# A four-layer residual network on one core: the residual kept doubled, ScalarE's gates opened in two parts, GpSimd's products held, another load order

## The reference

```
x = x + ssm(x)                       # conv over 16 rows of cond, softplus/tanh gates, a scan over time, 64 states
x = x + lstm(x, h0=cond)             # 512 steps; a = x_t Wx + h Wh + b; c = f c + i g; h = o tanh(c)
x = x + r * y                        # r = sigmoid(xr wr^T), xr = x + (xprev - x) maa_r
                                     # y: each token of xk = x + (xprev - x) maa_k through one of 16 experts
ax = abs(x); p = ax / sum_t(ax); pi = exp(2 p); th = pi / sum_t(pi)
chosen = sum_t(cumsum_t(th) + 0.001 <= cond); level = ax[chosen]
x = x + x * (ax >= level)            # so: x times 2 or times 1
```

## Time and profile before

| what | value |
|---|---|
| time, median of 3 | 4191.82 us (4191.44 to 4198.04) |
| profiled execution | 4197.63 us, of which span 4194.9 us |
| PE busy | 3890.3 us, 93% |
| DVE busy | 3109.5 us, 74% |
| ACT busy | 1679.4 us, 40% |
| POOL busy | 289.2 us, 7% |
| DMA | 267 MB, mean 64 GB/s |

### The profile page before, as it was taken

The page is one execution under the profiler, slowest core; times in us unless marked ns, Lnnn a source line. Parts: engine busy times, 40 slices in busy tenths (PEclk is TensorE's granted clock), DMA queues, the critical chain, the costliest instruction groups (busy, mean ns, idle before and its releaser), DMA issues. The chain is left out here.

```text
span 4194.9 us, 112126 instructions
## 1 busy us (share of the span) xinstructions
PE 3890.3 (93%) x44034; PEld 2542.4 (61%) x44034; DVE 3109.5 (74%) x10143; ACT 1679.4 (40%) x5296; POOL 289.2 (7%) x410
## 2 busy tenths in 40 slices
PE   3999999999999999999999999999599999996885
PEld 3566666666656666665666666665277888783332
DVE  9888888888878888887888888865455544544887
ACT  3334333334333333433333443333244434443554
POOL 2000000000000000000000000000000000002433
PEclk8999999999999999999999999999899999998887
DMA  7111111111111111111111111101233343324432
GB/s 282 27 37 27 27 34 27 34 37 27 27 35 27 32 34 31 27 34 27 27 32 38 27 27 34 22 17 20 79 148 121 139 158 122 120 83 148 148 133 71
DMA packets 388634, 266.97 MB, mean 64 GB/s; under 512 B 289721, under 2 KB 323001, under 8 KB 385060
## 3 DMA queue, kind: packets, MB, share of 16 engines
q1 hardware_dynamic: 366416, 184.21, 16.4%
q0 software_dynamic: 17696, 66.79, 4.2%
q10 hardware_dynamic: 4020, 9.10, 0.6%
HBM read 176.48 MB, written 83.92 MB: 62 GB/s over the span
## 5 line engine op out<-in xcount | busy, mean ns | idle before, releaser
L387 PE MATMUL bank<-buf,buf 128*16 128x256 f32 x32768 | 1874.2, 380 | 67.0 <-DVE buf L704 57.8
L387 PEld LDWEIGHTS bank<-buf,buf 128*16 128x16 f32 x32768 | 906.0, 97 | 890.8 <-DVE buf L704 88.9
L837 PE MATMUL bank<-buf,buf 128*128 128x256 f32 (+1 forms) x3072 | 1037.1, 338 | 4.0 <-DVE buf L1008 2.7
L838 PE MATMUL bank<-buf,buf 128*128 128x256 f32 (+1 forms) x3072 | 979.0, 319 | 0.0
L839 PE MATMUL bank<-buf,buf 128*128 128x256 f32 (+1 forms) x3072 | 978.4, 318 | 0.0
L597 DVE SCALAR_TENSOR_TENSOR buf<-buf,buf,buf 128x256 f32<-128x256 f32 x1920 | 870.9, 481 | 3.2 <-issue 3.2
L682 DVE STREAM_TRANSPOSE buf<-bank 128x256 f32<-128x256 f32 x1024 | 459.4, 449 | 421.7 <-PE bank L387 386.8
L554 ACT ACTIVATE buf<-buf 128x96 f32<-128x96 f32 x1024 | 290.5, 284 | 1146.5 <-DVE buf L687 1146.0
L837 PEld LDWEIGHTS bank<-buf,buf 128*128 128x128 f32 x3072 | 582.0, 189 | 254.6 <-issue 216.3
L839 PEld LDWEIGHTS bank<-buf,buf 128*128 128x128 f32 x3072 | 583.9, 190 | 41.2
L838 PEld LDWEIGHTS bank<-buf,buf 128*128 128x128 f32 x3072 | 584.7, 190 | 38.5
(11 more groups left out here) (137 smaller groups left out, 2977.4 us busy)
## 6 DMA issues: line engine op xcount, KB each, us to landing
buf<-in_wk SPq DMA_DIRECT2D x16, 2048.0 KB, 9.5
buf<-in_wv SPq DMA_DIRECT2D x16, 2048.0 KB, 9.3
buf<-in_xT SPq DMA_DIRECT2D x62, 496.0 KB, 3.8
buf<-in_xT SPq DMA_DIRECT2D x32, 512.0 KB, 3.6
expert_in_scratch<-buf POOLq DMA_DIRECT2D x16, 1024.0 KB, 22.7
x_scratch<-buf SPq DMA_DIRECT2D x32, 512.0 KB, 9.2
buf<-expert_in_scratch SPq DMA_DIRECT2D x16, 1024.0 KB, 11.5
expert_out_scratch<-buf POOLq DMA_DIRECT2D x64, 256.0 KB, 4.7
```

The source lines that it names most:

```text
L387: last = mm(gate_ps[hf][32 * j:32 * j + B, 0:HCOLS], hist[:, k, at_step(slot_at)], wh[:, k, j * GCOLS + hf * HCOLS:j * GCOLS + (hf + 1) * ...
L837: nc.tensor.matmul(out, left[0], right[0], start=first, stop=False)
L838: nc.tensor.matmul(out, left[0], right[1], start=False, stop=False)
```

## The change

The residual. From the first layer on, `stream`, x2 in DRAM and x3 are held doubled. To get there the output weights and bias of the first layer are doubled (`wo_pair`, `wo_rest`), x1 becomes 2 x center + out, the halo of the first tile is 2 x cond, and what reads the doubled x is halved: the scale of ScalarE's `keep_inputs`, maa_k and maa_r (`maa_last` = 0.5 maa, `maa_now` = 0.5 - 0.5 maa). Then `hist` (2h) is added as it is: `keep_x2` is one tensor_tensor over all four blocks, and x2_done counts 1 for it where it counted 4 (all waits on it are divided accordingly). In the finish the second half of `combine` is a plain addition and the multiplier is max(ax >= level, 0.5).

The input. `center` is loaded from a second copy of x, `xB`, which has the tile's steps innermost, batch by batch; the conv's window still reads `xT`.

The finish. ScalarE opens the gates 0 and 1 of row i+2 before `take_sides(i)` and the gates 2 and 3 after `absolute(i+1)`; in the run-in `exponent(0)` stands before the gates of row 1. GpSimd waits once for all four multipliers of a row, and then makes its four products. maa_r is loaded first, ScalarE no longer waits for wr, and the loads of rows 3 to 5 wait for the weighing of rows 0 to 2.

```diff
@@ -200,7 +200,7 @@
                     sp.sem_inc(s["sp_passed"], 1)
-                sp.dma_start(center, x_dram[:, :, bass.ds(m * LTILE, LTILE)]).then_inc(s["center_landed"], 16)
+                sp.dma_start(center, ins["xB"][:, :, bass.ds(m * LTILE, LTILE)]).then_inc(s["center_landed"], 16)
 
@@ -305,11 +305,11 @@
             pool.dma_start(y_d[E * CAP:E * CAP + 1, :], zeros[0:1, 0:D]).then_inc(s["zero_stored"], 16)
-            g.tensor_copy(stream[0][:, :, :, 0], cond).then_inc(s["halo_ready"], 1)
+            g.tensor_scalar(stream[0][:, :, :, 0], cond, 2.0, None, ALU.mult).then_inc(s["halo_ready"], 1)
 
...
                 if later(n, 1):
-                    pool.wait_ge(s["x2_done"], 2 * KD * n)
+                    pool.wait_ge(s["x2_done"], 2 * n)
                     pool.sem_inc(s["pool_passed"], 1)
@@ -489,17 +489,19 @@
                 a(xw[par][:, :, q, :], xw_ps[q % 2][:, 0:LTILE].rearrange("p (b t) -> p t b", b=B), ACT.Identity,
-                  bias=bias[:, q:q + 1]).then_inc(s["xw_ready"], 1)
+                  bias=bias[:, q:q + 1], scale=0.5).then_inc(s["xw_ready"], 1)
 
...
                     act.wait_ge(s["rows_turned"], r)
+                if not later(m, 1):
+                    act.wait_ge(s["share_ready"], 2)
                 act.wait_ge(s["halo_ready"], m + 1)
-                act.wait_ge(s["x2_done"], KD * (r + 1))
+                act.wait_ge(s["x2_done"], r + 1)
                 for k in range(KD):
                     a(mix[:, k, :].rearrange("p (b t) -> p b t", b=B), stream[four][:, k, :, 8 * u:8 * u + 8],
-                      ACT.Copy, scale=maa_k[:, k:k + 1])\
+                      ACT.Copy, scale=maa_last[:, k:k + 1])\
                         .then_inc(s["weighed"], 1)
@@ -519,8 +521,8 @@
             a(y_high[N_STATE:], ones[N_STATE:], ACT.Copy).then_inc(s["y_ones"], 1)
-            a(wo_pair, wo, ACT.Copy).then_inc(s["wo_high"], 1)
-            a(wo_rest[N_STATE:], bo_rows[N_STATE:], ACT.Copy).then_inc(s["wo_high"], 1)
+            a(wo_pair, wo, ACT.Copy, scale=2.0).then_inc(s["wo_high"], 1)
+            a(wo_rest[N_STATE:], bo_rows[N_STATE:], ACT.Copy, scale=2.0).then_inc(s["wo_high"], 1)
             for i, src in enumerate((dt_log, a_log)):
@@ -647,19 +649,17 @@
                     dve.wait_ge(s["halo_ready"], m - 2)
-                v.tensor_tensor(stream[four][:, two(q), :, 1:], out_ps[q].rearrange("p (k b t) -> p k b t", k=2, b=B),
-                                center[:, two(q), :].rearrange("p k (t b) -> p k b t", b=B),
-                                ALU.add).then_inc(s["x1_ready"], 1)
+                v.scalar_tensor_tensor(out=stream[four][:, two(q), :, 1:].rearrange("p k b t -> p (k b) t"),
+                                       in0=center[:, two(q), :].rearrange("p k (b t) -> p (k b) t", b=B), scalar=2.0,
+                                       in1=out_ps[q].rearrange("p (n t) -> p n t", t=LSTEPS), op0=ALU.mult,
+                                       op1=ALU.add).then_inc(s["x1_ready"], 1)
 
...
                 dve.wait_ge(s["h_ready"][1], LSTEPS * n + 8 * u + 9)
-                for k in range(KD):
-                    kept = stream[four][:, k, :, 8 * u + 1:8 * u + 9]
-                    last = v.scalar_tensor_tensor(
-                        out=kept, in0=hist[:, k, u * P:(u + 1) * P].rearrange("p (t b) -> p b t", b=B), scalar=0.5,
-                        in1=kept, op0=ALU.mult, op1=ALU.add)
-                    last.then_inc(s["x2_done"], 1)
+                kept = stream[four][:, :, :, 8 * u + 1:8 * u + 9]
+                v.tensor_tensor(kept, hist[:, :, u * P:(u + 1) * P].rearrange("p k (t b) -> p k b t", b=B), kept,
+                                ALU.add).then_inc(s["x2_done"], 1)
 
@@ -743,15 +744,18 @@
             dve.wait_ge(s["wo_high"], 2)
-            v.tensor_tensor(wo_rest[0:N_STATE], wo[0:N_STATE], wo_pair[0:N_STATE].bitcast(F32),
-                            ALU.subtract).then_inc(s["wo_ready"], 1)
-            v.tensor_tensor(wo_rest[BO_LOW:OUT_ROWS], bo_rows[BO_LOW:OUT_ROWS], wo_rest[BO_LOW:OUT_ROWS].bitcast(F32),
-                            ALU.subtract).then_inc(s["wo_ready"], 1)
+            v.scalar_tensor_tensor(out=wo_rest[0:N_STATE], in0=wo[0:N_STATE], scalar=2.0,
+                                   in1=wo_pair[0:N_STATE].bitcast(F32), op0=ALU.mult,
+                                   op1=ALU.subtract).then_inc(s["wo_ready"], 1)
+            v.scalar_tensor_tensor(out=wo_rest[BO_LOW:OUT_ROWS], in0=bo_rows[BO_LOW:OUT_ROWS], scalar=2.0,
+                                   in1=wo_rest[BO_LOW:OUT_ROWS].bitcast(F32), op0=ALU.mult,
+                                   op1=ALU.subtract).then_inc(s["wo_ready"], 1)
             dve.wait_ge(s["cond_landed"], 16)
...
                 convolve(0, q, 0, CONVS // 2)
-            v.tensor_scalar(maa_now, maa_k, -1.0, 1.0, ALU.mult, ALU.add).then_inc(s["share_ready"], 1)
+            v.tensor_scalar(maa_now, maa_k, -0.5, 0.5, ALU.mult, ALU.add).then_inc(s["share_ready"], 1)
+            v.tensor_scalar(maa_last, maa_k, 0.5, None, ALU.mult).then_inc(s["share_ready"], 1)
             dve.wait_ge(s["small_ready"], 4)
@@ -1075,10 +1080,12 @@
 
+            sp.dma_start(maa_r, ins["maa_r"]).then_inc(s["maa_landed"], 16)
             load(0)
-            sp.dma_start(maa_r, ins["maa_r"]).then_inc(s["weights_landed"], 16)
             sp.dma_start(wr, ins["wr"]).then_inc(s["weights_landed"], 16)
             for i in range(1, RING):
+                if i >= 3:
+                    sp.wait_ge(s["weighed"], KD * (i - 2))
                 load(i)
@@ -1122,8 +1130,8 @@
                     gather(i + 3)
-                for k in range(KD):
-                    pool.wait_ge(s["factor_ready"], KD * i + k + 1)
+                pool.wait_ge(s["factor_ready"], KD * (i + 1))
+                for k in range(KD):
                     if i >= 1:
@@ -1177,11 +1185,11 @@
                         act.wait_ge(s["xr_ready"], KD * (i - 1) + k + 1)
-                    a(weighed[:, k, :], stream[i % RING][:, k, 0:T], ACT.Copy, scale=maa_r[:, k:k + 1])\
+                    a(weighed[:, k, :], stream[i % RING][:, k, 0:T], ACT.Copy, scale=maa_last[:, k:k + 1])\
                         .then_inc(s["weighed"], 1)
 
-            def open_gate(i):
-                for m in range(KD):
+            def open_gate(i, first, last):
+                for m in range(first, last):
                     act.wait_ge(s["r_summed"], KD * i + m + 1)
@@ -1212,21 +1220,23 @@
 
-            act.wait_ge(s["weights_landed"], 32)
+            act.wait_ge(s["share_ready"], 1)
             weigh_last(0)
             weigh_last(1)
-            open_gate(0)
+            open_gate(0, 0, KD)
             weigh_last(2)
             absolute(0)
-            open_gate(1)
             exponent(0)
+            open_gate(1, 0, KD)
             weigh_last(3)
             for i in range(B):
+                if i + 2 < B:
+                    open_gate(i + 2, 0, 2)
                 take_sides(i)
...
                 if i + 2 < B:
-                    open_gate(i + 2)
+                    open_gate(i + 2, 2, KD)
                 if i + 1 < B:
@@ -1255,8 +1265,7 @@
                     dve.wait_ge(s["gated_ready"], u + 1)
-                    v.scalar_tensor_tensor(out=x2_of(i, k), in0=gated[k % 2], scalar=0.5, in1=x2_of(i, k),
-                                           op0=ALU.mult, op1=ALU.add).then_inc(s["x3_ready"], 1)
+                    v.tensor_tensor(x2_of(i, k), gated[k % 2], x2_of(i, k), ALU.add).then_inc(s["x3_ready"], 1)
 
@@ -1295,13 +1304,14 @@
                         dve.wait_ge(s["final_ready"], KD * (i - 1) + k + 1)
-                    v.tensor_scalar(factor[k], ax[i % 2][:, k, 0:T], column(level, i, k), 1.0, ALU.is_ge,
-                                    ALU.add).then_inc(s["factor_ready"], 1)
+                    v.tensor_scalar(factor[k], ax[i % 2][:, k, 0:T], column(level, i, k), 0.5, ALU.is_ge,
+                                    ALU.max).then_inc(s["factor_ready"], 1)
 
             v.tensor_scalar(rv, cond, -0.001, None, ALU.add).then_inc(s["rv_ready"], 1)
-            dve.wait_ge(s["weights_landed"], 32)
-            v.tensor_scalar(maa_now, maa_r, -1.0, 1.0, ALU.mult, ALU.add).then_inc(s["share_ready"], 1)
-            dve.wait_ge(s["share_ready"], 1)
+            dve.wait_ge(s["maa_landed"], 16)
+            v.tensor_scalar(maa_last, maa_r, 0.5, None, ALU.mult).then_inc(s["share_ready"], 1)
+            v.tensor_scalar(maa_now, maa_r, -0.5, 0.5, ALU.mult, ALU.add).then_inc(s["share_ready"], 1)
+            dve.wait_ge(s["share_ready"], 2)
             mix_in(0)
```

More of the change, by code:

```diff
@@ L119, in recur_phase @@
     wo_pair, wo_rest = carve(D, dt=F32R), carve(D, dt=F32R)
-    bias, conv_b, maa_k, maa_now = carve(NBLK), carve(KD), carve(KD), carve(KD)
+    bias, conv_b, maa_k, maa_last, maa_now = carve(NBLK), carve(KD), carve(KD), carve(KD), carve(KD)
     bp_b, bp_c, bs, a_log, dt_log = [carve(1)[0:N_STATE] for _ in range(5)]
@@ L233, in tile @@
```

(18 more changed lines are left out.)

## The result

The changed kernel takes 4120.86 us (4120.67 to 4122.64, 4 runs) against 4193.68 (4191.44 to 4198.04, 4 runs) for the one before: ratio 0.9826 (0.9809 to 0.9843), 72.8 us less. Forecast were 4141 us, with a range of 4114 to 4173. The direction and the range hold, but the time lies 20 us under the forecast. It is nearest to rival B (4118), whose rows of 17.4 to 17.6 us are nearly those of the trace (17.27). Of the two profiled executions, the spans are 4194.9 and 4117.7 us.

A forecast was written before the change was run, and what follows sets the result against it. VectorE was taken to bound the recurrence once per 16-step tile, and ScalarE's gate order to make it wait in finish rows. Terms -43.4, -23.4, +16.8, +6, -0.5, +1.2, -6.2, -1.3, +0.2 sum to -50.6 us: 4141, range 4114 to 4173.

The forecast's parts named there:

- rival B: Finish: products and gathers cost VectorE next to nothing; rows 17.4 to 17.6 us, sum -73.4, 4118 us; chance 0.20.
- (g): Recurrence: x2 in one instruction saves 0.20 us after step 15, 31 times, -6.2 us; after step 7 nothing.
- (a): Finish: opening ScalarE's gates in two parts removes VectorE's waits for the exponent, -43.4 us.
- Rival C: Finish: ScalarE reaches gates 0 and 1 before their blocks are done, wait stays; -7.2, 4185 us; chance 0.08.
- (b): Finish: holding GpSimd's products until all four multipliers saves 23.4 us; moved products delaying bound and combine cost +16.8 us.
- (c): Finish: gathers, moved over search and multipliers, cost 0.5 us a row, +6 us for 12 rows.
- Rival A: Finish: products and gathers both block VectorE, taking back the multipliers' gain; sum -22.6, 4169 us; chance 0.11.
- (d): Finish: the new multiplier and combine forms change nothing, 0, both ways within 0.01 x 64.
- (e): Finish's start: load order lets TensorE begin 3.7 us earlier, first row gives that back; -0.5 us, bounds -4 and +4.
- (f): Tail of the finish: the last row's products start only after all four multipliers, +1.2 us.
- (h): x1 from a centre in batch order: 0 in the recurrence, -1.3 us in the prologue; added maa_last costs 0.2.
- Rival D: Finish: TensorE's low clock lasts through its blocks, rows 23.8 us at clock 0.65; +14, 4206 us; chance 0.05.

The follow-up runs named there:

- the two single edits: Kernel before with only ScalarE's gates opened in two parts: 4149.29 us; kernel before with only GpSimd's products held until the fourth multiplier: 4192.16 us.

## Why the prediction was right, and where it was not

- *What bounds the kernel.* Right for the finish: it had its wait in ScalarE's order, and VectorE's work is the row once it is gone. In the recurrence VectorE is late at more steps than the one named, see (g).
- *(a)* Right, -43.5 alone. The timetable holds within 0.1 us at the turning's end; VectorE's wait is nil, ScalarE has 3.45 us in hand. Rival C, the wait that stays, is refuted.
- *(b), the saving.* Right in size: 1.67 for four, 24.2 us over the rows. It needs (a), which the two single edits show and the prediction did not say outright.
- *(b), the +16.8, and (c), the +6: the failed steps.* The prediction has "the four gathers queued ahead of them on GpSimd move too: they start when turning ends, at 15.1". They don't. `gather(i+3)` waits for `turned` at KD x (i+2), which is the turning of row i+1, done in the row before; that of row i+2 would be KD x (i+3). The trace of before had the sign of it: in rows 1 to 12 the first gather came behind the products, 0.81 us behind the end of a turning (4000.50 and 4001.31), and the turning that ends there, of row i+2, lets go `gather(i+4)`, which stands behind the products of row i. I read the release as one for gathers that stand ahead of them. With the gathers free to go behind the halo, the products stand first behind the multipliers and lie under the scans, and the gathers lie under combine, as they did before. The cost is 0.04 a row (the bound's 0.20 for 0.16) instead of 1.2 and 0.5. Of the 24.4 us by which rows 1 to 14 beat the sum, 22.8 are these two terms (less 0.6 for the bound); most of the rest is rows of 17.27 where 19.04 - 1.67 is 17.37, the next scan starting 0.09 before the last multiplier ends. So the mechanism was wrong here, and the range held because it took in rival B. The experiment with late gathers shows the predicted place to cost 29.5 us in all.
- *Rivals A and B.* B's time was nearly right, by another reason: the ports meet little because of when the work lies, not because a meeting is cheap. Rival A needed the gathers under the multipliers. Where they were put there, the multipliers kept their time and the gathers grew; so that a gather blocks the fast form is refuted, for gathers that started before the multipliers and among them. The Trainium skill (SBUF — State Buffer, Who interferes with whom) says that the pair is held for a whole instruction and the later one blocks fully: the gathers' growth agrees in kind, while the bound's 3.62 us, behind up to four products, is more than the one instruction that it speaks of.
- *(d)* Right: L1268 0.693, multipliers 0.48.
- *(e)* -0.5 predicted, +1.9 measured, within its bounds. Counted from the last transpose, TensorE did start earlier, by 3.3 of the 3.7 us. What was sized too small is the slow clock behind TensorE's 4.94 us wait: 10.12 us for the two blocks, which with 1.7 for the clock I gave 8.8 (and a clock of 0.67 in the second stretch of 3.4 us at the finish's start, where before had 0.98). The larger miss was not to price the exponent's place by itself: it costs 7.3.
- *(f)* +0.7 for +1.2.
- *(g)* -6.2 predicted; the median tile lost 0.26 us, 8.4 over 32. After step 15 it is 0.16 (0.20 predicted, 31 times, 5.0). After step 7 nothing was expected, as TensorE was read as the late one by 0.42; yet the transpose comes 0.22 earlier, and 0.13 of that is lost in the next step. That reading was wrong. TensorE's products of the step, before and after:
```profile
1063.86 3.65 PE L387 MATMUL bank<-buf,buf 128*16 128x256 f32 x64
```
```profile
1059.55 3.65 PE L387 MATMUL bank<-buf,buf 128*16 128x256 f32 x64
```
  In most steps of both kernels the transpose starts 2.85 us behind the first of these products, 0.07 behind the last one of its half: this is where TensorE is the late one. After step 7 it started 3.07 behind it before (1066.93) and starts 2.85 behind it now (1062.40). So 0.22 of the 0.42 idle was not TensorE's. It hangs on the one instruction (with four additions it is 3.07 again, 0.42 behind the last); what holds VectorE there, no trace shows. Only the first half gains so much: the second half's transpose comes 0.05 earlier, right behind TensorE's last product. Nor is step 15 the only other place: after step 5, in both kernels, the transpose stands on the end of `mix_in` with no wait, 0.18 later than 2.85.
- *(h)* Right: L652 at 0.680, nothing in the loop, -1.6 before the first transpose for -1.1. *(i)* Nothing seen.
- *Rival D, the clock.* Refuted: TensorE's wait fell to 1.53 us and the granted clock stayed full in the rows; over the stretch it rose from 0.89 to 0.93. But the earlier trace rows is only every second row of before. In the rows between, behind the same wait, the clock was 0.50 for 3.4 us and 0.67 in the next 3.4, and the same 16 records took 9.93 us instead of 8.81, which matches the 1.1 us by which the rows alternated (21.6 and 22.7):
```profile
3967.21 9.93 PE L1143 MATMUL bank<-buf,buf 128*128 128x512 f32 x16 [4.19 <-ACT buf L1188]
```

## What to carry to other kernels

Before moving a block of work on a queue, read the number that its wait compares with and name the row that it belongs to; a trace that shows who released it does not tell which iteration's signal it was. An idle time put down to an engine is not always that engine's: set the start against the engine's own work, in this step and in others. Price a wait's removal and a gain behind it together: the held products were worth 0 alone and 24 us once ScalarE was no longer late. And where an engine's filler ends right on the critical instruction, ask whether it can stand in a step with idle time before making it shorter: moving x2 brought 13.4 us, shortening it 6.5.
